# Selective scan on Trainium2: the old y is added by an identity product on TensorE, and ScalarE copies the sum into y

## Chip, cores and metric

One Trainium2 chip, one of its cores. The metric is the device time of one execution in microseconds. Engines are named as in the profile: PE is TensorE (PEld its weight loads), DVE is VectorE, ACT is ScalarE, POOL is GpSimd, SP is SyncE, which issues DMAs.

## What is computed

The program is a vision network of two layers over an image batch (2, 64, 64, 128). Layer 0 holds a convolution and four selective scans over 4096 positions and 256 channels with 16 states; layer 1 holds linear attention and a spectral filter. Only the scans are touched by the change:

```python
def step(h, inp):
    ut, dt, bt, ct = inp
    dA = jnp.exp(dt[..., None] * A4)
    h = dA * h + (dt * ut)[..., None] * bt[:, :, None, :]
    y = jnp.einsum('bkdn,bkn->bkd', h, ct)
    return (h, y)
...
y = out_y[:, 0] + inv_y[:, 0] + wh_y + invwh_y      # four orders summed back in place
```

Of the four scan orders (k = 0 to 3), k = 0 and 2 go over the rows of windows, k = 1 and 3 over the columns; k = 2 and 3 run backward. What each yields is added to one y of 256 channels by 4096 positions (two halves t of 128 channels, on 128 partitions).

## The kernel before

The scans of one image (function `scans`) run over k = 0 to 3 and over 8 chunks of L = 512 positions: 32 chunks an image, 64 in all. `chunk_stream` writes out the first and the last chunk of each k and loops over the others in pairs; every engine runs the same sequence of chunks with a body of its own, and semaphores alone tie them together. In a chunk there are 16 steps n, one for each state, with two halves t:

- ScalarE makes the decay of step n+2 (`decays`, L658) in its iteration n, as soon as VectorE has scanned step n, and every other iteration the scaled x of step n+3 (`times_b`, L649).
- TensorE drives step n+2 into the bank `p_drive` (`drive`: eight turns, L540, where n is even; eight products with a diagonal, L542, where it is odd), then adds what POOL has read out of step n-3 to the bank `p_y` (`sum_y`, L553).
- VectorE scans (`scan`, L762): state = decay * state + drive, 512 positions an instruction.
- POOL multiplies the state by C (`times_c`, L726) and keeps the carry (L730).

The work between chunks is strewn over these iterations. For the next chunk: TensorE projects at n = 0 (`project`, L496), makes the step products at n = 2 (L514), turns B at n = 9 (`turn_b`, L506) and x at n = 10 and 11 (L525); ScalarE takes the projection at n = 1, makes the step's parts at n = 4 (`step_parts`, L631 and L632), exp and ln at n = 6 (L636, L640); VectorE ends the step behind half of scan 8 (`finish_step`, L752); POOL multiplies it by u behind step 8 (L717).

For the chunk before: ScalarE copies its finished `p_y` to `y_tok` at n = 3 (`keep_y`, L672). TensorE turns its two halves into the bank `p_b`, half 0 at n = 6 and half 1 at n = 7 (`turn_y`, L567), each ahead of the drive of that iteration. There is one bank `p_b`: half 1 is turned only when half 0 has been taken out, and `turn_b` of the next chunk uses the same bank after that. VectorE takes the halves out (`add_y`, L777): y = y + bank, for half 0 behind scan (7, 0), for half 1 behind scan (9, 0). In k = 1 and 3 y is reached with a step of 64 positions (256 bytes), since the chunk lies along columns. The last chunk of an image (`c.last`) is ended behind its own steps. `begin_y` (L747) fills y with the skip terms ahead of the first scan and counts `y_begun`.

The semaphores that matter below: `y_kept` (keep_y is done), `y_turned` (a half is in the bank), `y_added` (the bank has been taken out), `scanned`, `driven`, `scaled`, `summed`, `read_out`.

Of the kernel before, what the change touches and what calls it, by code (L numbers as in the profile page):

```python
# [11 lines left out]
ALU = mybir.AluOpType  # L12
ACT = mybir.ActivationFunctionType
ds = bass.ds

P = 128
NB, H, W, C = 2, 64, 64, 128
# [5 lines left out]
L = 512  # L23
# [3 lines left out]
START = 16  # L27
# [372 lines left out]
def scans(nc, m, b):  # L400


    s = m.sem_b
    with ExitStack() as ctx:
# [13 lines left out]
        y_tok = sb("y_tok", [P, NB4, DI])  # L418
        carry = sb("carry", [P, NS, DT2])
        p_prep = ps("p_prep", [P, L])  # L420
        p_b = ps("p_b", [P, L])
# [10 lines left out]
        def flip(ap, c):  # L432
            return ap[:, ::-1] if c.backward else ap

        def following(c, nxt, n):
            return (c, n) if n < NS else (nxt, n - NS)

# [53 lines left out]
        def _(pe):  # L491
# [66 lines left out]
            def turn_y(c, t):  # L558

                if t == 0:  # L560
                    pe.wait_ge(s["y_kept"], START + c.g + 1)
                    pe.wait_ge(s["step_max"], START + c.g * 2 + (2 if c.last else 6 if c.following else 4))
                    pe.wait_ge(s["b_kept"], START + c.g + (1 if c.last else 2))
                else:
                    pe.wait_ge(s["y_added"], START + c.g * 2 + 1)
                for i in range(NB4):
                    last = pe.transpose(p_b[:, i * P:i * P + P], y_tok[:, i, t * P:t * P + P], m.ident[:, :])  # L567
                last.then_inc(s["y_turned"], 1)

            def body(c, nxt):  # L570
# [38 lines left out]
        @block.scalar  # L609
        def _(act):  # L610
            def keep_projection(c):
                act.wait_ge(s["projected"], START + c.g + 1)
                act.wait_ge(s["step_mm"], START + c.g * 2)
                act.wait_ge(s["b_turned"], START + c.g)
                act.wait_ge(s["c_stored"], START + c.g * 32)
                act.copy(xd[:, :], p_prep[:, :]).then_inc(s["xd_kept"], 1)

            def keep_b(c):
                act.wait_ge(s["b_turned"], START + c.g + 1)
                rows = p_b[:, :].rearrange("p (i r) -> p i r", r=P)[:, :, B_ROW:B_ROW + NS]  # L620
                act.copy(b_tok[:, c.parity, :, :], rows).then_inc(s["b_kept"], 1)

            def step_parts(c):
                if not c.first:
                    act.wait_ge(s["decay"], START + c.q * 2 + -2 * NS)
                act.wait_ge(s["x_turned"], START + c.g * 2)
                for t in range(DT2):
                    act.wait_ge(s["step_mm"], START + c.g * 2 + (t + 1))
                    bias = m.dt_b[:, DT2 * c.k + t:DT2 * c.k + t + 1]
                    bank = (p_prep, p_b)[t]  # L630
                    act.activation(softplus[:, t, :], bank[:, :], ACT.Abs, bias=bias).then_inc(s["step_abs"], 1)  # L631
                    act.activation(step[:, c.parity, t, :], bank[:, :], ACT.Relu, bias=bias).then_inc(s["step_max"], 1)  # L632

            def step_exp(c):
                act.wait_ge(s["step_abs"], START + c.g * 2 + 2)
                act.activation(softplus[:, :, :], softplus[:, :, :], ACT.Exp, scale=-1.0).then_inc(s["step_exp"], 1)  # L636

            def step_ln(c):
                act.wait_ge(s["step_exp"], START + c.g + 1)
                act.activation(softplus[:, :, :], softplus[:, :, :], ACT.Ln, bias=1.0).then_inc(s["step_ln"], 1)  # L640

            def times_b(c, n):
                if n == 0:
                    act.wait_ge(s["b_kept"], START + c.g + 1)
                    act.wait_ge(s["x_kept"], START + c.g * 2 + 2)
                if not (c.first and n < 2):
                    act.wait_ge(s["driven"], START + c.q * 2 + (2 * n - 2))
                for i in range(NB4):
                    last = act.activation(scaled[:, i, :], xu_tok[:, c.parity, i, :], ACT.Copy,  # L649
                                          scale=b_tok[:, c.parity, i, n:n + 1])  # L650
                last.then_inc(s["scaled"], 1)

            def decays(c, n, t):
                if n == 0:
                    act.wait_ge(s["step"], START + c.g + 1)
                if not (c.first and n < 2):
                    act.wait_ge(s["scanned"], START + c.q * 2 + (2 * n - 4 + t + 1))
                act.activation(decay[:, n % 2, t, :], step[:, c.parity, t, :], ACT.Exp,  # L658
                               scale=m.a_neg[:, DT2 * c.k + t, n:n + 1]).then_inc(s["decay"], 1)

            def keep_x(c, half):
                act.wait_ge(s["x_turned"], START + c.g * 2 + (half + 1))
                if not c.first:
                    act.wait_ge(s["scaled"], START + c.g * ODD + -ODD)
                    act.wait_ge(s["driven"], START + c.q * 2 + -2 * NS)
                act.copy(xu_tok[:, c.parity, 2 * half:2 * half + 2, :],
                         p_prep[:, :].rearrange("p (i d) -> p i d", d=DI)).then_inc(s["x_kept"], 1)

            def keep_y(c):
                act.wait_ge(s["summed"], START + c.q + NS)  # L670
                act.wait_ge(s["y_turned"], START + c.g * 2)
                act.copy(y_tok[:, :, :], p_y[:, :, :]).then_inc(s["y_kept"], 1)  # L672

            act.preload_act_table_set("natural_log_exp_and_others")
            preparation = {1: keep_projection, 4: step_parts, 11: keep_b}

            def body(c, nxt):
                if c.first:
                    keep_projection(c)
                    step_parts(c)  # L680
                    keep_b(c)
                    step_exp(c)
                    step_ln(c)
                    keep_x(c, 0)
                    keep_x(c, 1)
                    times_b(c, 0)
                    for n in range(2):
                        decays(c, n, 0)
                        decays(c, n, 1)
                    times_b(c, 2)  # L690
                for n in range(NS):
                    of, at = following(c, nxt, n + 2)
                    if of:
                        decays(of, at, 0)
                        decays(of, at, 1)
                    of, at = following(c, nxt, n + 3)
                    if of and at % 2 == 0:
                        times_b(of, at)
                    if n == 3 and not c.first:
                        keep_y(Before(c))  # L700
                    if nxt and n in preparation:
                        preparation[n](nxt)
                    if nxt and n == 6:
                        step_exp(nxt)
                        step_ln(nxt)
                    if nxt and n in (10, 12):
                        keep_x(nxt, n // 2 - 5)
                if c.last:
                    keep_y(c)

            chunk_stream(act, b, body)

        @block.gpsimd
# [29 lines left out]
        def _(dve):  # L743
# [19 lines left out]
                                       flip(p_drive[:, n % 2, t, :], c), 0.0 if c.start else carry[:, n, t:t + 1],  # L763
                                       ALU.mult, ALU.add).then_inc(s["scanned"], 1)

            def add_y(c, t):

                dve.wait_ge(s["y_turned"], START + c.g * 2 + (t + 1))
                dve.wait_ge(s["y_added"], START + c.g * 2 + t)
                dve.wait_ge(s["y_begun"], START + b * 2 + 2)  # L770
                if c.k % 2 == 0:
                    y, p = m.y[:, t, ds(c.at, L)], p_b[:, :]
                else:
                    column = (c.at // W)
                    y = m.y[:, t, :].rearrange("p (h w) -> p w h", w=W)[:, ds(column, L // H), :]
                    p = p_b[:, :].rearrange("p (w h) -> p w h", h=H)
                dve.tensor_tensor(y, y, p, ALU.add).then_inc(s["y_added"], 1)  # L777

            def body(c, nxt):
                if c.first:  # L780
                    begin_y(0)
                    finish_step(c)
                    begin_y(1)
                for n in range(NS):
                    scan(c, n, 0)
                    if n in (7, 9) and not c.first:
                        add_y(Before(c), n // 2 - 3)
                    if nxt and n == 8:
                        finish_step(nxt)
                    scan(c, n, 1)  # L790
                if c.last:
                    add_y(c, 0)
                    add_y(c, 1)

            chunk_stream(dve, b, body)


# [1289 lines left out]
```

## Time and profile before

| | us |
|---|---|
| median of 3 runs (6186.34 to 6195.12) | 6189.54 |
| the profiled execution | 6196.9 |
| span of the profiled execution, first to last instruction | 6195.1 |
| PE busy | 5676.1 (92%) |
| DVE busy | 4384.0 (71%) |
| ACT busy | 3169.3 (51%) |
| POOL busy | 3095.3 (50%) |

The span covers all of the program; the two images' scans lie at about 210 to 1650 us and 1910 to 3340 us, the spectral filter behind them takes most of the rest. Shares over the span are means over these stages, so the scan is read by itself below. In the views, a line of a timeline gives the start, the duration, the engine, the line of the program, the operation, output and inputs, the number of instructions that were merged, and in brackets the idle time ahead of it with what ended it. Durations of merged instructions overlap a little with the next line, so lengths are taken from start to start.

### The profile page before, as it was taken

The page shows a single profiled execution, that of the slowest core. Times are in us where ns is not written, and L with a number is a line of the kernel's source. Part 1 is how long each engine was busy: PE and PEld are TensorE (multiplying, and loading weights), DVE is VectorE, ACT ScalarE, POOL GpSimd, SP SyncE. Part 2 cuts the span into 40 slices and gives each one's busy share as a digit, 9 for nine tenths or more (in the row PEclk, how much of TensorE's full clock was granted, in tenths as well). Part 3 has the DMA queues.
Part 4 walks back from the last instruction along what each step waited for, and adds up shares of the span by engine and source line. Part 5 has one row for each costly group of instructions (what it writes and reads, how often), then busy time and mean ns, then how long its engine had stood idle before and what let it go on. Part 6 is the DMA issues. An engine that isn't in the chain of part 4 may idle for free. (4 is left out here: it accounts for less than half of the span.)

```text
span 6195.1 us, 128742 instructions
## 1 busy us (share of the span) xinstructions
PE 5676.1 (92%) x41691; PEld 5066.6 (82%) x41691; DVE 4384.0 (71%) x5986; ACT 3169.3 (51%) x6029; POOL 3095.3 (50%) x2015
## 2 busy tenths in 40 slices
PE   7899999999888999999998667999999989999998
PEld 5688888888766888888886546999989879999987
DVE  2699999999717999999996664555555555555554
ACT  2699888988737998899886321111111111111110
POOL 1699999999717999999996301111111101111110
PEclk9899999999998999999999888999999999999999
DMA  2455555555414555555554237777766666777765
GB/s 97 109 145 141 141 140 142 140 145 141 128 60 121 143 145 139 139 144 144 142 141 123 56 99 173 156 152 151 152 153 154 167 152 149 154 155 159 153 151 146
DMA packets 1098946, 858.33 MB, mean 139 GB/s; under 512 B 305622, under 2 KB 1021238, under 8 KB 1064374
## 3 DMA queue, kind: packets, MB, share of 16 engines
q1 hardware_dynamic: 1097974, 844.72, 55.1%
q10 hardware_dynamic: 720, 10.49, 0.4%
q8 instruction: 130, 2.13, 0.1%
q14 instruction: 122, 1.00, 0.1%
HBM read 811.50 MB, written 43.55 MB: 138 GB/s over the span
## 5 line engine op out<-in xcount | busy, mean ns | idle before, releaser
L726 POOL TENSOR_TENSOR read<-state,c_wide 128x1024 f32<-128x1024 f32 x1024 | 2419.9, 2380 | 216.7 <-DVE state L762 129.0
L762 DVE TENSOR_TENSOR_SCAN state<-decay,carry,p_drive 128x512 f32<-128x512 f32 x1792 | 2140.9, 1259 | 103.9 <-PE p_drive L540 57.1
L658 ACT ACTIVATE decay<-step,a_neg 128x512 f32<-128x512 f32 x2048 | 1398.2, 717 | 225.1 <-DVE state L762 215.9
L1747 PE MATMUL p_y<-window,x_high 128*128 128x256 f32 x7936 | 1490.8, 286 | 0.0
L1811 ACT COPY term_blocks<-p_s 128x256 f32<-128x256 f32 x832 | 310.5, 373 | 2096.2 <-PE p_s L1747 2096.2
L1747 PEld LDWEIGHTS p_y<-window,x_high 128*128 128x128 f32 x7936 | 1239.1, 191 | 0.0
L1747 PE MATMUL p_y<-window,x_low 128*128 128x256 f32 x3968 | 1130.5, 285 | 0.0
L553 PE MATMUL p_y<-ident,read 128*128 128x128 f32 x8192 | 1064.1, 273 | 13.0 <-ACT y_tok L672 3.7
L542 PE MATMUL p_drive<-diag_b,xu_tok 128*128 128x128 f32 x8192 | 1004.0, 276 | 1.3 <-DVE state L762 1.3
L542 PEld LDWEIGHTS p_drive<-diag_b,xu_tok 128*128 128x128 f32 x8192 | 960.5, 193 | 1.6 <-DVE state L762 1.6
L553 PEld LDWEIGHTS p_y<-ident,read 128*128 128x128 f32 x8192 | 925.2, 141 | 25.4 <-issue 21.7
L649 ACT ACTIVATE scaled_x<-xu_tok,b_tok 128x256 f32<-128x256 f32 x2048 | 868.1, 496 | 74.9 <-PE p_drive L540 74.7
L1747 PEld LDWEIGHTS p_y<-window,x_low 128*128 128x128 f32 x3968 | 755.8, 190 | 0.0
L1842 POOL TENSOR_TENSOR mix_weights<-mix_weights,frac_filter 128x512 f32<-128x512 f32 x64 | 73.2, 1144 | 1318.3 <-PE p_mix L1785 1311.0
L540 PE MATMUL p_drive<-ident,scaled_x 128*128 128x128 f32 x4096 | 562.2, 278 | 114.6 <-ACT scaled_x L649 97.2
L540 PEld LDWEIGHTS p_drive<-ident,scaled_x 128*128 128x128 f32 x4096 | 452.8, 142 | 254.4 <-issue 144.6
L1747 PE MATMUL p_s<-window,x_high 128*128 128x256 f32 x2432 | 531.6, 306 | 80.6 <-DMA window<-taps_scratch 45.4
L1880 DVE TENSOR_TENSOR term_blocks<-p_y,term_blocks 128x512 f32<-128x512 f32 x384 | 265.6, 692 | 391.0 <-PE p_y L1747 383.4
L1834 POOL TENSOR_TENSOR mix_weights<-mix_weights 128x512 f32<-128x512 f32 x64 | 82.5, 1290 | 893.0 <-DMA mix_weights<-in_M_minus 890.5
L1747 PEld LDWEIGHTS p_s<-window,x_high 128*128 128x128 f32 x2432 | 390.3, 191 | 136.0 <-issue 97.1
L1785 PE MATMUL p_mix<-term_blocks,mix_weights 128*128 128x512 f32 (+1 forms) x1280 | 461.2, 507 | 1.9 <-DVE term_blocks L1863 1.9
L1862 DVE TENSOR_TENSOR term_blocks<-p_y,term_blocks 128x256 f32<-128x256 f32 x448 | 186.3, 416 | 356.5 <-PE p_y L1747 355.4
(257 smaller groups left out, 6023.7 us busy)
## 6 DMA issues: line engine op xcount, KB each, us to landing
c_wide<-c_scratch SPq DMA_DIRECT2D x256, 1024.0 KB, 4.7
window<-taps_scratch SPq DMA_DIRECT2D x576, 257.0 KB, 6.5
diag_b<-diag_scratch SPq DMA_DIRECT2D x256, 512.0 KB, 4.1
window<-taps_scratch SPq DMA_DIRECT2D x768, 129.0 KB, 5.3
window<-taps_scratch SPq DMA_DIRECT2D x128, 513.0 KB, 7.1
window<-taps_scratch SPq DMA_DIRECT2D x64, 385.0 KB, 6.1
gate_scratch<-gate_out SPq DMA_DIRECT2D x16, 512.0 KB, 3.1
gate_in<-gate_scratch SPq DMA_DIRECT2D x8, 1024.0 KB, 6.0
```

The lines of the kernel that those rows point to most:

```text
L540: last = pe.transpose(o, scaled[:, i, t * P:t * P + P], m.ident[:, :])
L542: last = pe.matmul(o, xu_tok[:, c.parity, i, t * P:t * P + P], diag[:, n // 4 % 2, n // 2 % 2, i, :], start=True, stop=True)
L553: last = pe.matmul(p_y[:, i, t * P:t * P + P], read[:, n % 4, t, i * P:i * P + P], m.ident[:, :], start=n == 0 and i % 2 == 0 and t == 0, ...
L649: last = act.activation(scaled[:, i, :], xu_tok[:, c.parity, i, :], ACT.Copy, scale=b_tok[:, c.parity, i, n:n + 1])
L658: act.activation(decay[:, n % 2, t, :], step[:, c.parity, t, :], ACT.Exp, scale=m.a_neg[:, DT2 * c.k + t, n:n + 1]).then_inc(s["decay"], 1)
L726: pool.tensor_tensor(read[:, n % 4, :, :], state[:, n % 4, :, :], wide, ALU.mult).then_inc(s["read_out"], 1)
L762: dve.tensor_tensor_scan(flip(state[:, n % 4, t, :], c), flip(decay[:, n % 2, t, :], c), flip(p_drive[:, n % 2, t, :], c), 0.0 if c.start ...
L1747: last = pe.matmul(out, x[:, source, blk, :], view[:, :, at:at + P][:, :, ::-1], start=first and x is m.x_high and z == 0, stop=True, skip ...
L1785: last = pe.matmul(p_mix[par][:, at:at + size], mix_now[:, kind, reach, :], filtered[:, j % 2, par ^ kind, kind, at:at + size], start=kind ...
L1811: act.copy(shared[:, i % 4, :, :], shared_bank(i)).then_inc(s["kept"], 1)
L1862: dve.tensor_tensor(to[:, :, 0:P], half_of(p_y[i % 4], 0), shared[:, i % 4, :, :], ALU.add)
L1880: dve.tensor_tensor(to.rearrange("p k (h t) -> p k h t", h=2), p_y[i % 4][:, :].rearrange("p (h k t) -> p k h t", h=2, k=2), out.rearrange ...
```

## The change

On TensorE `turn_y` puts the old y into the bank first, as a product with the identity (one 128x128 by 128x512 product, start of the accumulation), and the four turns then accumulate onto it. ScalarE gets a new function `end_y`, which copies the bank into y, in its iterations n = 7 and n = 8 behind decays and `times_b`. VectorE's `add_y` is gone with its two calls. The meaning of `y_added` stays (the bank has been taken out), but ScalarE counts it now. `y_of` is the address of a chunk's half in y.

```diff
+        def y_of(c, t):
+
+            if c.k % 2 == 0:
+                return m.y[:, t, ds(c.at, L)]
+            column = (c.at // W)
+            return m.y[:, t, :].rearrange("p (h w) -> p w h", w=W)[:, ds(column, L // H), :]
...
             def turn_y(c, t):
...
                 else:
                     pe.wait_ge(s["y_added"], START + c.g * 2 + 1)
+                pe.wait_ge(s["y_begun"], START + b * 2 + 2)
+                old = y_of(c, t)
+                bank = p_b[:, :] if c.k % 2 == 0 else p_b[:, :].rearrange("p (w h) -> p w h", h=H)
+                pe.matmul(bank, m.ident[:, :], old, start=True, stop=False, skip_group_check=True)
                 for i in range(NB4):
-                    last = pe.transpose(p_b[:, i * P:i * P + P], y_tok[:, i, t * P:t * P + P], m.ident[:, :])
+                    last = pe.matmul(p_b[:, i * P:i * P + P], y_tok[:, i, t * P:t * P + P], m.ident[:, :], start=False,
+                                     stop=True, is_transpose=True, skip_group_check=True)
                 last.then_inc(s["y_turned"], 1)
...
+            def end_y(c, t):
+
+                act.wait_ge(s["y_turned"], START + c.g * 2 + (t + 1))
+                src = p_b[:, :] if c.k % 2 == 0 else p_b[:, :].rearrange("p (w h) -> p w h", h=H)
+                act.copy(y_of(c, t), src).then_inc(s["y_added"], 1)
...
                     if n == 3 and not c.first:
                         keep_y(Before(c))
+                    if n in (7, 8) and not c.first:
+                        end_y(Before(c), n - 7)
...
                 if c.last:
                     keep_y(c)
+                    end_y(c, 0)
+                    end_y(c, 1)
...
-            def add_y(c, t):
-
-                dve.wait_ge(s["y_turned"], START + c.g * 2 + (t + 1))
-                dve.wait_ge(s["y_added"], START + c.g * 2 + t)
-                dve.wait_ge(s["y_begun"], START + b * 2 + 2)
...
-                dve.tensor_tensor(y, y, p, ALU.add).then_inc(s["y_added"], 1)
...
                 for n in range(NS):
                     scan(c, n, 0)
-                    if n in (7, 9) and not c.first:
-                        add_y(Before(c), n // 2 - 3)
                     if nxt and n == 8:
                         finish_step(nxt)
                     scan(c, n, 1)
-                if c.last:
-                    add_y(c, 0)
-                    add_y(c, 1)
```

## Rows read from the trace of the kernel before

**Rows 1.** Busy us and count of PE, PEld, DVE, ACT, POOL; clock; DMA: scan stretch

```profile
215.00:580.00 365.00, 349.21 (x2820) 316.33 (x2820) 338.14 (x285) 329.03 (x613) 340.19 (x204) 0.99 0.52 141
```

**Rows 2.** Timeline of VectorE: its first sums of chunks 1 and 31

```profile
278.04 0.69 DVE L777 TENSOR_TENSOR y<-y,p_b 128x512 f32 x1 [0.72 <-PE p_b L567]
...
1623.33 1.33 DVE L777 TENSOR_TENSOR y<-y,p_b 128x512 f32<-128x512 f32 x1 [0.77 <-PE p_b L567]
```

**Rows 3.** Timeline of ScalarE in one chunk of k=0

```profile
402.31 1.70 ACT L649 ACTIVATE scaled_x<-xu_tok,b_tok 128x256 f32<-128x256 f32 x4 [1.18 <-PE p_drive L540]
...
415.67 1.69 ACT L649 ACTIVATE scaled_x<-xu_tok,b_tok 128x256 f32<-128x256 f32 x4
417.26 1.58 ACT L658 ACTIVATE decay<-step,a_neg 128x512 f32<-128x512 f32 x2
...
446.67 1.71 ACT L649 ACTIVATE scaled_x<-xu_tok,b_tok 128x256 f32<-128x256 f32 x4 [1.18 <-PE p_drive L540]
```

**Rows 4.** Timeline of TensorE in the same chunk

```profile
411.40 1.09 PE L540 MATMUL p_drive<-ident,scaled_x 128*128 128x128 f32 x8 [0.43 <-ACT scaled_x L649]
412.32 1.04 PE L553 MATMUL p_y<-ident,read 128*128 128x128 f32 x8
413.19 0.60 PE L567 MATMUL p_b<-ident,y_tok 128*128 128x128 f32 x4
413.63 1.95 PE L542 MATMUL p_drive<-diag_b,xu_tok 128*128 128x128 f32 x16
415.42 1.04 PE L553 MATMUL p_y<-ident,read 128*128 128x128 f32 x8
417.49 1.31 PE L540 MATMUL p_drive<-ident,scaled_x 128*128 128x128 f32 x8 [1.03 <-ACT scaled_x L649]
...
419.89 0.66 PE L506 MATMUL p_b<-ident,xd 128*128 128x128 f32 x4 [0.22 <-DVE y L777]
420.38 1.95 PE L542 MATMUL p_drive<-diag_b,xu_tok 128*128 128x128 f32 x16
...
437.42 1.88 PE L496 MATMUL p_prep<-s,xproj 128*128 x4
439.13 1.04 PE L540 MATMUL p_drive<-ident,scaled_x 128*128 128x128 f32 x8
```

**Rows 5.** Groups by shape, whole span: VectorE's sums; busy us, mean ns, idle before

```profile
L777 DVE TENSOR_TENSOR y<-y,p_b 128x512 f32 x96 | 94.7, 986 | 33.7 <-PE p_b L567 33.7
...
L777 DVE TENSOR_TENSOR y<-y,p_b 128x512 f32<-128x512 f32 x32 | 31.3, 979 | 22.9 <-PE p_b L567 22.9
```

**Rows 6.** Timeline of VectorE in the chunk of rows 3, end of the step

```profile
414.57 2.33 DVE L752 TENSOR_TENSOR step<-step,shared 128x1024 f32<-128x1024 f32 x1 [0.23 <-ACT shared L640]
```

**Rows 7.** Groups, whole span: ScalarE's copies out of a bank; busy us, mean ns

```profile
L666 ACT COPY xu_tok<-p_prep 128x512 f32<-128x512 f32 x128 | 72.4, 566 | 29.4 <-PE p_prep L525 29.4
...
L314 ACT ACTIVATE s<-pc,conv_b 128x512 f32 x32 | 36.1, 1129 | 0.0
...
L312 ACT ACTIVATE s<-pc,conv_b 128x512 f32 x32 | 22.0, 688 | 110.3 <-PE pc L285 110.2
```

**Rows 8.** One line, 580 to 940 us (k=1): duration ns min/median/max, starts

```profile
L777 DVE TENSOR_TENSOR y<-y,p_b x16: 656/1262/1360, 588.5 to 914.5; 128x512 f32 x12, 128x512 f32<-128x512 f32 x4
```

**Rows 9.** Columns of rows 1: pauses of TensorE and the 5 us after

```profile
3389.36:3392.65 3.29, 0.00 (x1) 0.00 (x1) 1.63 (x2) 1.52 (x2) 2.73 (x2) 1.00 0.20 59
3392.65:3397.65 5.00, 4.10 (x32) 3.72 (x32) 1.29 (x2) 0.00 (x0) 2.25 (x1) 1.00 0.23 66
...
3502.72:3506.47 3.75, 0.00 (x0) 0.00 (x1) 3.75 (x21) 2.50 (x5) 1.54 (x2) 1.00 0.00 0
3506.47:3511.47 5.00, 5.00 (x27) 4.53 (x28) 2.35 (x12) 0.32 (x2) 0.96 (x1) 0.66 0.00 0
...
3764.22:3769.17 4.95, 0.00 (x0) 0.03 (x1) 3.97 (x5) 0.00 (x0) 4.46 (x6) 0.73 0.86 147
3769.17:3774.17 5.00, 5.00 (x26) 5.00 (x27) 0.71 (x3) 0.40 (x2) 0.40 (x1) 0.59 0.99 271
```

More of the change, by code:

```diff
@@ L764, in scan @@
                                        ALU.mult, ALU.add).then_inc(s["scanned"], 1)
-            def add_y(c, t):
-                dve.wait_ge(s["y_turned"], START + c.g * 2 + (t + 1))
-                dve.wait_ge(s["y_added"], START + c.g * 2 + t)
-                dve.wait_ge(s["y_begun"], START + b * 2 + 2)
[L771 to L776, printed above, removed]
-                dve.tensor_tensor(y, y, p, ALU.add).then_inc(s["y_added"], 1)
             def body(c, nxt):
```

## The prediction

> **What bounds the kernel now.** I read first the busy time by engine inside the scan, then the length of one chunk, then one chunk in order of time on each engine. The busy times name no single bound: in a 365 us stretch of the scan TensorE is busy 349 us, POOL 340, VectorE 338 and ScalarE 329 [rows 1]. So a gain on VectorE isn't a gain by itself. VectorE's first sum of the first chunk starts at 278.04 and that of the thirty-first at 1623.33, which makes 44.84 us for a chunk [rows 2].
>
> The order of time shows a ring. In a chunk of stage k=0, ScalarE can start `times_b` of step 6 at 402.31, when TensorE has driven step 4; from there it runs without a pause (times_b, keep_y, decays, step_parts, decays, times_b, decays, exp, ln, decays, times_b) until 417.26, 14.95 us [rows 3]. TensorE waits for the end of that: its drive of step 10 starts at 417.49 with a wait of 1.03 us on ScalarE. Then come sum_y, turn_b and, from 420.38, the drive of step 11 and all that follows without any pause worth naming [rows 4], until the next chunk's drive of step 4 lets ScalarE start `times_b` of step 6 again, at 446.67 [rows 3]. So a round is 14.95 us of ScalarE, 3.12 us in between (417.26 to 420.38) and 26.29 us of TensorE (420.38 to 446.67): 44.36 us. Every link is a semaphore or the order on one engine. VectorE is in the ring only for a moment: `turn_b` waits for its second sum, 0.22 us [rows 4].
>
> **What leaves VectorE.** 128 sums, 94.7 + 31.3 = 126.0 us, and the waits ahead of them, 33.7 + 22.9 = 56.6 us [rows 5]. At most 183 us would come back if VectorE were the ring. It isn't: after the first sum VectorE runs two scans and then waits for ScalarE's ln, 0.23 us [rows 6]; without the sum it arrives earlier and waits longer. I count the removal at 0 and what hides it is ScalarE's 14.95 us.
>
> **What the identity products cost.** Nothing in the trace multiplies the identity by 512 columns, but `project` does two full 128x128 by 128x512 products between 437.42 and 439.13, 0.86 us each [rows 4]. Two a chunk. The first, in `turn_y(0)`, falls ahead of drive 8, for which TensorE waits 0.43 us for ScalarE now [rows 4]: 0.86 - 0.43 = 0.43 us of delay, and that is absorbed, because TensorE waits for ScalarE a little later in any case. Without that cover it would be 0.86 x 60 = 52 us. The second is in the ring (below).
>
> **What the copies cost on ScalarE.** The copy of 128x512 out of a bank is 0.57 us [rows 7]. In the stages k=1 and 3 it writes y with a step of 256 bytes. The nearest row for a stepped write is the second Silu, which writes the column order and takes 1.129 us where the first, from the same bank, takes 0.688 [rows 7]: +0.44 us. VectorE's sum read and wrote with that step and cost no more at its quickest, 0.656 us in k=1 against 0.69 in k=0 [rows 2, 8]. I take +0.44 for ScalarE (between 0 and 0.88) and 0 for the product's reading of the old y (between 0 and +0.86, a doubling). The Trainium skill's page "SBUF — State Buffer" (section "Door 1: The DMA port swizzle") says that a step beyond 16 bytes loses bandwidth on each access. ScalarE's rows agree with that, VectorE's do not; by the rule the product pays too, which is the upper end just named.
>
> **The wait that the change puts in.** This is the term that decides. `turn_y(1)` has to wait until the bank is free. Before, VectorE freed it right after scan 7: at 413.19 TensorE starts the second turn without a wait and does drive 9 (413.63 to 415.42) and sum_y 4 while ScalarE is still busy [rows 4]. After, the bank is freed by `end_y(0)`, which stands in ScalarE's program behind decays and `times_b` of step n=7, so at 417.26, the end of the 14.95 us. TensorE is in order: behind its wait stand drive 9, sum_y 4, drive 10, sum_y 5, turn_b, drive 11. Worked out on the same chunk, from 417.26:
> copy 0.57 [rows 7], semaphore 0.13 (as from the end of `times_b`, 415.67 + 1.69, to drive 10 at 417.49) [rows 3, 4], product 0.86, four turns 0.44 (413.19 to 413.63), drive 9 1.79, sum_y 4 0.87 (412.32 to 413.19), drive 10 0.87 (eight transposes as well), sum_y 5 0.87, turn_b 0.49 (419.89 to 420.38) [rows 4]. Sum 6.89 us in place of 3.12. The round becomes 14.95 + 6.89 + 26.29 = 48.13 us. Who waits behind it: VectorE's scan 9 (needs drive 9), POOL's step 8 (needs sum_y 4, some 3.6 us later than now), then everybody.
>
> Against the mean of 44.84 that is +3.29 us a chunk. Thirty chunks of each of the two images have the full round: +197 us. Of these 60, 28 belong to k=1 or 3: 28 x 0.44 = +12. The last chunk and the two closing turns of each image have the products without the ring; I put +5 for all of that.
>
> **TensorE's clock.** The new wait makes TensorE idle from the end of sum_y 3 (413.19 now, about 413.6 with the first product ahead of it) to 417.96: 4.4 us a chunk, more where the copy is stepped. In the scan the granted clock is 0.99 of full [rows 1]. Elsewhere in this trace TensorE had such pauses: after 3.75 us without a product the clock of the next 5 us was 0.66, after 4.95 us it was 0.59, while after 3.29 us it stayed 1.00 [rows 9]. The 0.66 is a stretch at 1.2 GHz among 2.4 GHz. A clock of 0.66 over 5 us of dense work loses 5 x 0.34 = 1.7 us, 0.59 loses 2.05. Whatever is lost there lies in the ring, right behind the wait. I take 1.7 us: 60 x 1.7 = +102 us, with bounds 0 and 60 x 2.05 = 123. The Trainium skill's page "TensorE: Matmul & The Clock Gate" (section "HAM oscillation — how this bites in real kernels") tells of a kernel that waits between bursts and is throttled anew in every round, which speaks against this change. The rows named agree with it, except that no scan chunk here has had such a pause yet.
>
> **The sum.** 197 + 12 + 5 + 102 = +316 us. The profiled execution took 6196.9 us, so 6513; it lies 7.4 us above the median of the runs, so 6189.5 + 316 = 6505 us.
>
> **Rivals.**
> Clock stays up: the pause is there but the clock holds, as after 3.29 us [rows 9]. Then 197 + 12 + 5 = 214, 6404 us; without the stepped write 6392. For it: the pause of 3.29 us kept the clock. Against it: ours lies between the two that lost it. Chance 0.19.
> The wait is hidden (the other side): if ScalarE reached `end_y(0)` before TensorE has finished sum_y 3, that is 4 us earlier than its rows say, the ring would be as now and TensorE's own work would decide: 349.2/365 x 44.84 = 42.9 us [rows 1] and two products of 0.86, 44.6 us a chunk, -0.2 x 60 = -14 us, 6175 us. It decides from the point where the 14.95 us shrink below 11. Nothing on ScalarE is removed, so I see no way: 0.03 for it and 0.02 for a mixture that ends within 0.2%.
> Stepped accesses are dear: product at four times 0.86 in the second turn, 2.6 x 28 = +72, and the copy at +0.88, another +12: 6589 us. Chance 0.06. For it: ScalarE's stepped write; against it: VectorE's sums.
> Smaller slowdown, under 6385: ScalarE's stretch or TensorE's 26.29 us has slack which the rows don't show. Chance 0.03.
> The forecast itself: 0.67.
>
> **How the numbers follow.** The range goes from 6385 (clock holds, no stepped write, 6392, less the spread of the runs) to 6590 (clock 123, the product doubled in the stepped chunks +24, the copy +25, semaphores of 0.3 us more a round +18, from 6189.5 + 202: 6582). Outside remain the two cases of hidden waits, the smaller slowdown and a part of the dear accesses. About 0.2% can be told from no change here: faster by over that 0.03, within it 0.02, slower 0.95.
>
> **What would show it.** In the profile after: TensorE's second turn (the product on the identity ahead of the turns) waits some 4 us for ScalarE's copy into y in nearly every chunk; that copy starts without a pause behind `times_b`; a chunk lasts 49 to 51 us by its copies; granted clock in the scan 0.95 to 0.97 instead of 0.99, low right behind the wait; VectorE idle 8 us or more a chunk, with drive 9 as the releaser. A chunk of 48.1 us at full clock would be the first rival. The forecast is wrong if TensorE's wait ahead of the second turn is under 2 us, or if the chunks stay near 44.8 us: then ScalarE doesn't run without pause up to `end_y(0)`, and the ring isn't what I read.

## The result and the profile after

The change makes the kernel slower: 6565.3 us (median of four runs, 6564.6 to 6572.2) against 6189.8 (four runs, 6186.3 to 6195.1). The ratio is 1.061, 95% interval 1.059 to 1.062. The profiled execution took 6572.2 us where the one of before took 6196.9: +375.3 us. The forecast was +316 us, 6505 us in a range of 6385 to 6590.

The busy time of the engines over the whole span, in the profile after (us, share of the span, count):

```profile
PE 5925.9 (90%) x41947; PEld 5228.4 (80%) x41947; DVE 4331.5 (66%) x5858; ACT 3272.6 (50%) x6157; POOL 3094.2 (47%) x2015
```

TensorE has 128 products (256 records) more and is busy 250 us longer, far more than 128 products of 0.86 us = 110 us. The stretches of time, in the columns of [rows 1], first the stretch of the scan, then five pieces of one chunk of k=0:

```profile
215.00:580.00 365.00, 335.00 (x2554) 299.93 (x2553) 300.23 (x243) 302.01 (x562) 304.21 (x183) 0.94 0.48 125
...
418.85:430.21 11.36, 11.25 (x97) 10.47 (x94) 10.56 (x9) 11.10 (x20) 10.31 (x7) 1.00 0.88 140
430.21:434.76 4.55, 0.17 (x2) 0.01 (x1) 3.74 (x3) 4.52 (x10) 3.48 (x2) 0.90 0.21 58
434.76:437.48 2.72, 2.72 (x7) 1.58 (x7) 0.33 (x1) 1.10 (x2) 0.00 (x0) 0.50 0.69 289
437.48:440.77 3.29, 3.29 (x17) 3.29 (x17) 1.18 (x1) 0.59 (x1) 0.00 (x0) 0.52 0.00 0
440.77:443.83 3.06, 3.06 (x31) 3.06 (x29) 2.75 (x4) 2.26 (x5) 1.94 (x1) 1.00 0.00 0
```

Every engine does less in 365 us than in [rows 1], since fewer chunks fit into the stretch. In the chunk, TensorE has almost nothing to do for 4.55 us, and then works without a gap for 6.01 us (434.76 to 440.77) at a granted clock of 0.50 to 0.52, that is 1.2 GHz in place of 2.4.

What TensorE waits for there stands in its timeline of the same chunk (start, duration, line, operation, count, and in brackets the idle time ahead and what ended it):

```profile
427.17 1.02 PE L576 MATMUL p_b<-y,ident 128*128 x2
428.03 0.60 PE L578 MATMUL p_b<-ident,y_tok 128*128 128x128 f32 x4
428.46 1.04 PE L547 MATMUL p_drive<-ident,scaled_x 128*128 128x128 f32 x8
429.34 1.04 PE L560 MATMUL p_y<-ident,read 128*128 128x128 f32 x8
434.76 2.07 PE L576 MATMUL p_b<-y,ident 128*128 x2 [4.38 <-ACT y L685]
436.62 1.06 PE L578 MATMUL p_b<-ident,y_tok 128*128 128x128 f32 x4
437.48 3.46 PE L549 MATMUL p_drive<-diag_b,xu_tok 128*128 128x128 f32 x16
...
443.83 1.95 PE L549 MATMUL p_drive<-diag_b,xu_tok 128*128 128x128 f32 x16
```

and ScalarE's, from `times_b` of step 6 in this chunk to the same instruction in the next:

```profile
419.11 1.71 ACT L661 ACTIVATE scaled_x<-xu_tok,b_tok 128x256 f32<-128x256 f32 x4 [1.13 <-PE p_drive L547]
...
432.46 1.69 ACT L661 ACTIVATE scaled_x<-xu_tok,b_tok 128x256 f32<-128x256 f32 x4
434.06 0.56 ACT L685 COPY y<-p_b 128x512 f32 x1
...
437.81 0.59 ACT L685 COPY y<-p_b 128x512 f32 x1 [1.95 <-PE p_b L578]
...
470.15 1.70 ACT L661 ACTIVATE scaled_x<-xu_tok,b_tok 128x256 f32<-128x256 f32 x4 [1.15 <-PE p_drive L547]
```

In [rows 4] the second turn at 413.19 started without a wait. Now the product ahead of it stands 4.38 us for ScalarE's copy, and the copy starts at 434.06 without a pause behind `times_b`, 14.95 us after 419.11. From the copy to drive 11 it is 9.77 us (434.06 to 443.83), where before it was 3.12 from the end of `times_b`. From there to the next `times_b` of step 6 it is 26.32 us; before it was 26.29.

The table of waits of the whole program, three of its lines (who waits at which line, for what; us in total, count, longest):

```profile
POOL read L748 <- PE p_y L560: 566.0, 246, 8.1
DVE state L784 <- PE p_drive L549: 278.5, 138, 5.2
...
PE p_b L576 <- ACT y L685: 256.4, 64, 4.4
```

TensorE's wait occurs ahead of the second half of all 64 chunks, 4.0 us in the mean. The waits of VectorE for the drives and of POOL for `p_y` are for the most part the same delay, seen by those who stand behind TensorE.

### The profile page after: what moved, and what is told of

Read it like the earlier page. It is cut to its first block and busy times, and to the rows that moved or that the text cites. A ratio compares the mean times of both kernels' runs of the same rounds, so it can differ in the third digit from the quotient of the medians.

```text
span 6570.4 us, 129250 instructions
## 1 busy us (share of the span) xinstructions
PE 5925.9 (90%) x41947; PEld 5228.4 (80%) x41947; DVE 4331.5 (66%) x5858; ACT 3272.6 (50%) x6157; POOL 3094.2 (47%) x2015
## 5 line engine op out<-in xcount | busy, mean ns | idle before, releaser
L784 DVE TENSOR_TENSOR_SCAN state<-decay,carry,p_drive 128x512 f32<-128x512 f32 x1792 | 2167.3, 1264 | 503.3 <-PE p_drive L549 251.4
L549 PE MATMUL p_drive<-diag_b,xu_tok 128*128 128x128 f32 x8192 | 1077.1, 288 | 0.0
L549 PEld LDWEIGHTS p_drive<-diag_b,xu_tok 128*128 128x128 f32 x8192 | 1039.5, 206 | 0.0
L1751 PE MATMUL p_s<-window,x_high 128*128 128x256 f32 x2432 | 530.7, 306 | 81.6 <-DMA window<-taps_scratch 46.4
L547 PE MATMUL p_drive<-ident,scaled_x 128*128 128x128 f32 x4096 | 541.4, 275 | 9.8 <-ACT scaled_x L661 8.7
L576 PE MATMUL p_b<-y,ident 128*128 (+1 forms) x256 | 224.3, 968 | 259.1 <-ACT y L685 256.4
```

Of the source, the lines that this page charges most:

```text
L547: last = pe.transpose(o, scaled[:, i, t * P:t * P + P], m.ident[:, :])
L549: last = pe.matmul(o, xu_tok[:, c.parity, i, t * P:t * P + P], diag[:, n // 4 % 2, n // 2 % 2, i, :], start=True, stop=True)
L576: pe.matmul(bank, m.ident[:, :], old, start=True, stop=False, skip_group_check=True)
L784: dve.tensor_tensor_scan(flip(state[:, n % 4, t, :], c), flip(decay[:, n % 2, t, :], c), flip(p_drive[:, n % 2, t, :], c), 0.0 if c.start ...
L1751: last = pe.matmul(out, x[:, source, blk, :], view[:, :, at:at + P][:, :, ::-1], start=first and x is m.x_high and z == 0, stop=True, skip ...
```

## Experiments

Two theories to begin with. **The place of the copy**: the one bank `p_b` couples TensorE's second product to `end_y(0)`, which ScalarE reaches only at the end of its 14.95 us; the low clock follows from that wait. **The work**: 128 products and 128 copies were put on engines that had none to spare, and would cost the same wherever they stood. The chunks below are measured from one copy of `p_y` into `y_tok` to the next. The columns by k give the commonest length, the means are over 30 chunks of the first image, and the last column is the interval ahead of its closing copy. The ratios are to runs of the kernel before taken beside each run (medians of 6188.3 to 6192.9 us). In the kernel after, the first, the thirty-first and the closing one of these copies in ScalarE's timeline:

```profile
269.32 0.99 ACT L690 COPY y_tok<-p_y 128x1024 f32<-128x1024 f32 x1
...
1795.29 0.99 ACT L690 COPY y_tok<-p_y 128x1024 f32<-128x1024 f32 x1
1835.55 1.01 ACT L690 COPY y_tok<-p_y 128x1024 f32<-128x1024 f32 x1 [10.37 <-PE p_y L560]
```

(1795.29 - 269.32) / 30 = 50.87 us, and 1835.55 - 1795.29 = 40.3. Not all chunks of the kernel after have the commonest length: some are 49.4 to 50.9 us.

| kernel | us | ratio to before (95%) | chunk, k=0, 2 | chunk, k=1, 3 | mean | last |
|---|---|---|---|---|---|---|
| before | 6189.8 | | 44.4 | 45.6 | 44.85 | 33.8 |
| after | 6565.3 | 1.061 (1.059 to 1.062) | 51.1 | 51.15 | 50.87 | 40.3 |
| fill_pause | 6446.8 | 1.041 (1.040 to 1.043) | 48.2 | 49.5 | 48.76 | 39.2 |
| no_product | 6474.2 | 1.045 (1.044 to 1.047) | 48.9 and 50.1 | 49.0 and 50.1 | 49.56 | 36.2 |
| vector_copies | 6256.2 | 1.011 (1.009 to 1.013) | 45.0 | 46.4 | 45.76 | 35.8 |
| early_copy | 6203.7 | 1.002 (1.001 to 1.003) | 44.5 | 45.4 | 44.88 | 37.9 |
| two_banks | 6204.4 | 1.002 (1.001 to 1.003) | 44.5 | 45.4 | 44.89 | 38.1 |
| before_two_banks | 6190.9 | 1.000 (0.999 to 1.001) | 44.4 | 45.6 | 44.87 | 33.8 |
| late_second_sum | 6190.4 | 1.000 (0.999 to 1.001) | 44.4 | 45.6 | 44.87 | 33.7 |
| pool_step_first | 6189.2 | 1.000 (0.999 to 1.001) | 44.4 | 45.6 | 44.84 | 33.7 |
| two_banks_pool_first | 6166.3 | 0.996 (0.994 to 0.997) | 44.0 | 45.0 | 44.38 | 36.2 |

In no_product a shorter and a longer chunk mostly follow each other by turns, whatever the k; why was not traced.

**fill_pause: keep TensorE at work in the pause.** Behind sum_y 3 TensorE does four products into `p_prep`, which is free there; nothing reads them.

```diff
+ if n == 6 and not c.first:
+     for i in range(4):
+         pe.matmul(p_prep[:, :], m.ident[:, :], y_tok[:, 0:2, :], start=True, stop=True)
```

> The changed kernel, with four more products of 128x512 on TensorE (identity times y_tok, 0.86 us each, into the bank p_prep that is free then) behind sum_y 3 of n=6, in the pause ahead of the second turn; nothing reads what they write. Theory (the pause lets the clock fall, and that costs 2.9 us a chunk behind the pause): the clock in the scan goes back to 0.98 or more, the stretch from the copy to drive 11 shrinks from 9.8 us to about 6.9 in k=0; chunks of 48.1 us in k=0 and 2, 49.4 in k=1 and 3; 6189 + 197 + 12 + 24 + 5 = 6430 us, 6400 to 6460. Rival (TensorE has too much work, the clock is only a sign of it): more work makes it slower still, 6565 us or above.

Measured: 6446.8 us, 118 us less than after, with more work. Stretch of the scan and timeline of TensorE, with the added products first:

```profile
215.00:580.00 365.00, 355.07 (x2685) 308.31 (x2685) 309.89 (x250) 313.57 (x582) 313.33 (x188) 0.99 0.50 131
```

```profile
424.82 3.60 PE L614 MATMUL p_prep<-y_tok,ident 128*128 128x512 f32 x8
...
429.36 1.12 PE L576 MATMUL p_b<-y,ident 128*128 x2 [0.94 <-ACT y L688]
430.32 0.60 PE L578 MATMUL p_b<-ident,y_tok 128*128 128x128 f32 x4
430.76 1.95 PE L549 MATMUL p_drive<-diag_b,xu_tok 128*128 128x128 f32 x16
...
435.60 1.95 PE L549 MATMUL p_drive<-diag_b,xu_tok 128*128 128x128 f32 x16
```

The clock is back at 0.99 and the product takes 0.96 us to the turns in place of 1.86. So the low clock costs 118 us, and the rest of the slowdown, 257 us, is there at full clock. The wait for the copy is still what holds TensorE. The copy starts at 428.66 here and drive 11 at 435.60, 6.94 us later, where the forecast had 6.89; the chunk is 48.2 us, where it had 48.13.

**no_product: the wait without the product.** The turns start the bank, and the old y isn't added; ScalarE copies as in the kernel after.

```diff
- pe.matmul(bank, m.ident[:, :], old, start=True, stop=False, skip_group_check=True)
- last = pe.matmul(p_b[...], y_tok[...], m.ident[:, :], start=False, stop=True, is_transpose=True, ...)
+ last = pe.transpose(p_b[...], y_tok[...], m.ident[:, :])
```

> The changed kernel without the identity products: the four turns start the bank themselves, ScalarE copies the bank into y as before, so y holds only the last order's part at each place (the old y isn't added). Theory (the wait for ScalarE's copy, and the clock behind it, are the cost): the pause stays, some 5.2 us now, and the clock falls all the same; of the 6.1 us a chunk about 1.9 go, the product at half clock: 6440 to 6490 us. Rival (the products themselves are the cost): 6190 to 6250 us.

Measured: 6474.2 us. The second half's turns in the timeline:

```profile
433.60 1.12 PE L575 MATMUL p_b<-ident,y_tok 128*128 128x128 f32 x4 [4.51 <-ACT y L681]
```

The pause is as long without the product (4.51 us; some 5.2 were expected), and three quarters of the slowdown stay (284 of 376 us). Taking the products away gives back 91 us; that they cost this only where they stand behind the wait is seen from the experiments that follow.

**vector_copies: the product without ScalarE's copies.** VectorE copies the bank into y at the two places where it added before.

```diff
- if n in (7, 8) and not c.first: end_y(Before(c), n - 7)          # ScalarE
+ if n in (7, 9) and not c.first: take_y(Before(c), n // 2 - 3)    # VectorE, dve.tensor_copy
```

> The changed kernel with its products, but VectorE copies the bank into y, at the places where its sums stood (behind scan 7 and scan 9 of half 0). Theory: no pause of TensorE above 2 us, the clock stays at 0.99, the ring is that of the kernel before; the two products fill TensorE's 1.5 us of slack a chunk and go a little over it, by 0.3 us in k=0 and 2 and by 1.9 in k=1 and 3, where the stepped product takes 1.70: 6250 us, 6220 to 6290. Rival (products are the cost): 6400 or more. Rival (VectorE's time is what counts): like before, 6190.

Measured: 6256.2 us, 309 us less than after, with all 128 products in it. TensorE's two products of a chunk of k=1 have no wait:

```profile
640.02 1.88 PE L576 MATMUL p_b<-y,ident 128*128 x2
...
643.91 1.88 PE L576 MATMUL p_b<-y,ident 128*128 x2
```

Here it is VectorE's second copy that holds TensorE up, ahead of `turn_b`:

```profile
651.69 0.66 PE L513 MATMUL p_b<-ident,xd 128*128 128x128 f32 x4 [0.58 <-DVE y L787]
```

So the slowdown hangs on who empties the bank, and when. The two experiments that follow leave the work where the change has put it, and take away only the place or only the shared bank.

**early_copy: the first copy one iteration sooner.** `end_y(0)` goes from behind `times_b` at n=7 to n=6, between decays and exp; nothing else changes.

```diff
- if n in (7, 8) and not c.first:
-     end_y(Before(c), n - 7)
+ if n in (6, 8) and not c.first:
+     end_y(Before(c), n // 2 - 3)
```

> The changed kernel with the first copy moved in ScalarE's program from behind times_b of n=7 to n=6, behind its decays and ahead of exp; same work on every engine. Theory: the bank is free when TensorE reaches the second turn, no pause, clock 0.99, and the ring is 44.1 us in k=0 and 2, with TensorE's work (44.6 and, with the stepped product, 46.3) as the bound: 6200 to 6260 us. Rival (ScalarE's added work, or TensorE's, is the cost): stays within 50 us of 6565.

**two_banks: the second half into another bank.** Half 1 goes to `p_prep`, so it needn't wait for the copy of half 0; `turn_b` then waits for the first copy alone and the turn of x for both.

```diff
- pe.wait_ge(s["y_added"], START + c.g * 2 + 1)       # turn_y, t = 1
+ pe.wait_ge(s["y_added"], START + c.g * 2)
...
+ p_half = (p_b, p_prep)[t]
```

> The changed kernel with the second half turned into the bank p_prep, which is free from step_parts to turn_x: the second turn then waits for no copy. turn_b waits for the first copy, turn_x for the second. Theory: the wait itself is gone and with it the pause and the fall of the clock; TensorE's work is the bound, 44.6 us a chunk in k=0 and 2 and 46.3 in k=1 and 3 (stepped product 1.70): 6230 us, 6190 to 6260. Rival (ScalarE's added copies lengthen its stretch): 6300 or more.

Measured: 6203.7 and 6204.4 us, the same within their intervals. TensorE's second product of a chunk of k=0 has no wait, in early_copy and in two_banks:

```profile
413.75 1.02 PE L576 MATMUL p_b<-y,ident 128*128 x2
```

```profile
412.93 1.02 PE L577 MATMUL p_prep<-y,ident 128*128 x2
```

Moving one copy of 0.56 us gives back 362 of the 376 us. The work theory has fallen: products and copies are all still there, and the chunk is 44.9 us as before. In k=1 and 3 it is 45.4 us, where both expectations had put TensorE's work at 46.3. Of what stays, some 14 us, the last chunks of the images make up 6: they are 4.1 to 4.3 us longer in the first image and 1.9 in the second. The rest was not traced.

But why is neither faster than before, with 126 us of sums [rows 5] gone from VectorE? In two_banks TensorE is busy 357 of 365 us in k=0 and 298 of 300 in k=1 (stretches of time):

```profile
215.00:580.00 365.00, 356.99 (x2844) 320.67 (x2844) 331.50 (x271) 334.88 (x626) 340.31 (x204) 0.99 0.54 141
600.00:900.00 300.00, 297.99 (x2331) 261.51 (x2330) 274.64 (x221) 276.89 (x510) 277.91 (x168) 1.00 0.54 140
```

That looks like TensorE at its end. The same question was put to the kernel before, by taking away in turn what TensorE waits for there.

**before_two_banks: the same two banks in the kernel before.** VectorE's sums stay; `turn_b` no longer waits for the second one.

```diff
- pe.wait_ge(s["y_added"], START + (c.g * 2 + -2))    # turn_b
+ pe.wait_ge(s["y_added"], START + (c.g * 2 + -3))
...
+ p_half = (p_b, p_prep)[t]                            # turn_y; add_y reads the same
```

> The kernel before, unchanged but for the banks: the second half is turned into p_prep, turn_b waits for the first sum alone, turn_x for both. Theory (in the kernel before VectorE's second sum is in the ring, by turn_b's wait of 0.2 us in k=0 and 2 and 0.8 in k=1 and 3): 32 x 0.2 + 28 x 0.8 = 29 us less, 6160, 6150 to 6185. Rival (other waits take its place): 6185 to 6195.

**late_second_sum: besides, VectorE's second sum one scan later.**

```diff
- if n in (7, 9) and not c.first: add_y(Before(c), n // 2 - 3)
+ if n in (7, 10) and not c.first: add_y(Before(c), n // 10)
```

> The kernel before with the second half in p_prep, as in before_two_banks, and VectorE's second sum moved from behind scan (9, 0) to behind scan (10, 0), since in before_two_banks TensorE's drive 11 waits 0.70 us for scan 9, which stands behind that sum. Theory (the second sum is in the ring through scan 9): drive 11 starts 0.4 us earlier in k=0 and 2 and up to 1.0 us earlier in k=1 and 3: 32 x 0.4 + 28 x 1.0 = 41 us less, 6150, 6140 to 6175. Rival (POOL's read-out or the next wait takes it): 6180 to 6195, and then VectorE's sums cost nothing where they stand.

**pool_step_first: besides, POOL multiplies the step by u ahead of its eighth read** in place of behind it.

```diff
+ if nxt and n == 8: step_times_u(nxt)
  times_c(c, n)
- if nxt and n == 8: step_times_u(nxt)
```

> late_second_sum with POOL's product of the next step and u taken ahead of its read-out of step 8 instead of behind it. Theory (in late_second_sum TensorE waits 0.4 us for that product ahead of turn_x: a second path, ln, end of the step, scan 8, read-out 8, that product, turn_x, is as long as the one through turn_b; POOL stands idle 1.38 us ahead of read-out 8, so the product fits in there): now both paths are shorter and the 0.4 to 1.0 us a chunk that late_second_sum was to gain appear: 6150 us, 6135 to 6175. Rival (a third path, POOL's own 41 us a chunk or VectorE's scans, takes over at once): 6180 to 6195.

Measured: 6190.9, 6190.4 and 6189.2 us: all three as before. My expectation of a gain missed three times. Each time the wait taken away is gone, and another stands close by. In before_two_banks drive 11 waits for VectorE:

```profile
873.43 1.16 PE L543 MATMUL p_drive<-diag_b,xu_tok 128*128 128x128 f32 x8 [0.70 <-DVE state L763]
```

In late_second_sum that is gone too, and the turn of x waits for POOL's product, which stands behind its read:

```profile
873.10 0.65 PE L526 MATMUL p_prep<-ident,shared 128*128 128x128 f32 x4 [0.40 <-POOL shared L718]
```

In pool_step_first POOL's product comes early. VectorE's second sum stands in the same chunk's timeline without a wait, and VectorE scans on from there for 17.67 us without a pause:

```profile
418.89 2.37 POOL L718 TENSOR_TENSOR shared<-step,s 128x1024 f32<-128x1024 f32 x1
```

```profile
423.33 0.66 DVE L779 TENSOR_TENSOR y<-y,p_prep 128x512 f32 x1
423.91 17.67 DVE L763 TENSOR_TENSOR_SCAN state<-decay,carry,p_drive 128x512 f32<-128x512 f32 x15
```

By these waits, three paths through a chunk are equally long to within a microsecond: ScalarE's stretch and the turns on TensorE; ln, the end of the step, scan 8 and POOL's read and product; and VectorE's own scans and sums. This is read from the waits; no run takes away the third path alone.

**two_banks_pool_first: the same move of POOL in two_banks**, where VectorE's sums are gone as well.

```diff
+ if nxt and n == 8: step_times_u(nxt)                 # POOL, two_banks otherwise
  times_c(c, n)
- if nxt and n == 8: step_times_u(nxt)
```

> two_banks (the changed kernel without the wait) with the same move on POOL. Theory (there TensorE's own work is the bound, 44.5 us a chunk at 98% busy in k=0 and 2 and 45.4 at 99% in k=1 and 3): nothing to gain, 6195 to 6210 us. Rival (POOL's path bounds it too): 6160 to 6185, and then the change can pay.

Measured: 6166.3 us, 38 us less than two_banks and faster than both kernels (0.996, 0.994 to 0.997). The rival won, by which TensorE with 98% of busy time was not yet the bound. TensorE's turn of x, two_banks first:

```profile
422.88 0.65 PE L533 MATMUL p_prep<-ident,shared 128*128 128x128 f32 x4 [0.39 <-POOL shared L741]
```

and two_banks_pool_first:

```profile
419.91 0.60 PE L533 MATMUL p_prep<-ident,shared 128*128 128x128 f32 x4
```

The wait is gone, and in its k=1 TensorE is now busy for all but 0.8 of 300 us. With the wait for the copy and POOL's path out of the way, the change as a whole (VectorE's sums gone, products and copies added) is worth 23 us against pool_step_first (6189.2 to 6166.3). How much VectorE's part alone is worth hangs on what else there is: with the products in place, taking the copies from VectorE to ScalarE's early place gave 52 us (vector_copies to early_copy).

## Why the prediction came out as it did

**The ring: right, to the hundredth in its untouched parts.** ScalarE's 14.95 us, now 419.11 to 434.06, and TensorE's stretch, 26.32 for 26.29, are as read. The step that decides, `end_y(0)` at the end of ScalarE's stretch and TensorE in order behind it, is shown by early_copy: one copy moved, 362 us back.

**The wait, +197 us: right in size.** At full clock the part in between is 6.94 us for 6.89, and the chunk of k=0 is 48.2 for 48.13 (fill_pause). Against the mean of before, (48.2 - 44.85) x 60 = 201. The forecast, too, compared the ring of k=0 with the mean over all k, and so its +197 holds two things that it does not name. Stage by stage the chunk grows by 3.8 us in k=0 (44.4 to 48.2) and 3.9 in k=1 (45.6 to 49.5); 3.8 x 60 = 228. Against that stands the longer ring that k=1 and 3 had before, where VectorE's sums have the step: TensorE waits there for a scan that stands behind the first sum, and longer than in k=0 for the second sum. In a chunk of k=1 of the kernel before:

```profile
868.06 0.66 PE L540 MATMUL p_drive<-ident,scaled_x 128*128 128x128 f32 x4 [0.60 <-DVE state L762]
...
870.40 0.66 PE L506 MATMUL p_b<-ident,xd 128*128 128x128 f32 x4 [0.81 <-DVE y L777]
```

By these waits it is 0.60 + 0.81 - 0.22 = 1.2 us, the 45.6 against 44.4 of the table; with the sums these 28 x 1.2 = 34 us leave the ring, and 228 - 34 = 194.

**The stepped accesses, +12: too small, and one row was misread.** The chunk of k=1 in fill_pause is 1.3 us longer than that of k=0; over 28 chunks that is 36 us. The copy was sized well. The step that failed is the product's reading of the old y with a step, taken as 0 from VectorE's rows with an upper end of a doubling. VectorE's rows do not say 0. The quickest sum of [rows 8], 0.656 us, stands at the head of that window: it is a sum of the last chunk of k=0, which has no step. VectorE's timeline before, with it and the first sum of k=1:

```profile
596.44 0.66 DVE L777 TENSOR_TENSOR y<-y,p_b 128x512 f32<-128x512 f32 x1
632.85 1.35 DVE L777 TENSOR_TENSOR y<-y,p_b 128x512 f32 x1 [0.77 <-PE p_b L567]
```

In the first image VectorE's sums take 0.65 to 0.69 us without the step and 1.24 to 1.36 with it; [rows 2] has one of each. Read so, the row would have given the product about its upper end, 28 x 0.86 = 24 us more. It is a doubling for TensorE as well. Timeline of TensorE in a chunk of k=1 of the kernel after, first product and second:

```profile
731.28 1.88 PE L576 MATMUL p_b<-y,ident 128*128 x2
732.98 0.62 PE L578 MATMUL p_b<-ident,y_tok 128*128 128x128 f32 x4
...
739.32 2.07 PE L576 MATMUL p_b<-y,ident 128*128 x2 [3.98 <-ACT y L685]
741.21 1.04 PE L578 MATMUL p_b<-ident,y_tok 128*128 128x128 f32 x4
```

From start to start the first takes 1.70 us; in k=0 it took 0.86 (427.17 to 428.03). The Trainium skill's page "SBUF — State Buffer", section "Door 1: The DMA port swizzle", has every access that goes on to a new line of 16 bytes pay a penalty. TensorE's 1.70 us at full clock, ScalarE's copies and VectorE's sums agree with it, against what the forecast says of VectorE.

**The clock, +102: the mechanism right, the term too small and its shape wrong.** fill_pause shows 118 us between the two kernels, and by the chunks (50.87 - 48.76) x 60 = 127. The forecast put 1.7 us into every chunk. In chunks of the commonest length it is 2.9 in k=0 (51.1 - 48.2) and 1.65 in k=1 (51.15 - 49.5), and over all chunks 2.1 in the mean. The granted clock of the scan is 0.94, where the forecast had 0.95 to 0.97. For k=0 the failing step was to take the deficit from stretches of 5 us [rows 9]. The low clock lies on TensorE's work from 434.76 to 440.77, and that work takes 6.01 us where the same instructions take 0.86 + 0.44 + 1.79 = 3.09 at full clock. In other chunks the clock comes back sooner. One of the soonest behind an unstepped product, kernel after, columns as in [rows 1], the product with its turns and then drive 9:

```profile
587.99:590.71 2.72, 2.72 (x6) 1.58 (x7) 0.41 (x1) 1.18 (x2) 0.00 (x0) 0.50 0.73 304
590.71:592.55 1.84, 1.84 (x17) 1.84 (x17) 0.53 (x1) 0.59 (x1) 0.00 (x0) 0.97 0.00 0
```

For k=1 the stepped product hides part of the loss: at 1.2 GHz it takes 1.89 us (739.32 to 741.21), and that is hardly more than the 1.86 of the unstepped one (434.76 to 436.62). So the step and the low clock do not add up there: in the kernel after itself the product's step costs the ring next to nothing, as forecast, but by luck, since it is the low clock that hides it.

**The ends, +5: too small.** The last interval of an image is 40.3 us for 33.8, twice 6.5 = 13. There the copies and turns stand one behind the other; early_copy still has 4.1 of the 6.5 in the first image and 1.9 in the second.

Together by the chunks: 201 + 36 + 127 + 13 = 377, measured 376. By the runs themselves fill_pause splits it as 257 + 118; the chunks would have 250 + 127. Of the difference of some 8 us, 1.4 lie in the last interval of fill_pause's second image (41.7 us, where after has 40.3); the rest I didn't trace.

**VectorE's sums, counted at 0: right in k=0, for a wider reason.** I gave ScalarE's 14.95 us as what hides them; in k=1 and 3 the sums put the 1.2 us named above into the ring of before, which the mean as base took in unnamed. The experiments on the kernel before show that POOL's path and VectorE's own hide as well, within a microsecond. That `turn_b` waits 0.22 us for the second sum had no price either: with that wait gone (before_two_banks) nothing changed.

**The rivals.** "Clock stays up" is fill_pause, where it was forced: 6447, not 6404. The stepped product (28 x 0.84 = 24) and the ends (5.3 and 7.9, forecast 5) account for 32 of the 43 us; the rest I didn't trace. "The wait is hidden" is early_copy and two_banks: 6204, not 6175, as TensorE's busy time does not decide while POOL's product still holds up the turn of x. With that out of the way it is 6166, under the 6175 that TensorE's busy time was taken to allow.

## What to carry to other kernels

When a step goes to another in-order engine, look first at which instruction frees the buffer that it shares, and at the place of that instruction in its engine's order: one copy of 0.56 us, one iteration too late, cost 362 us, and a free bank or an earlier place gave them back. Here TensorE's waits of 3.9 to 4.4 us cost more than their length, since the work behind them was done at the lower clock; price that by the work that lies in the low stretch. Before a minimum or a median of a window is used as a price, look at which instruction it belongs to: a window that began one chunk too early made a doubled access look free. Where removing a wait brings nothing, the next path is as long: remove waits together, and don't take 98% of busy time for the bound before the last wait is gone.

## What the runs showed of the hardware

- TensorE's clock was 0.50 behind pauses of 3.9 to 4.4 us in the scan and full again some 3 to 6 us after the work had started anew, so it was lost in every chunk. The Trainium skill's page "TensorE: Matmul & The Clock Gate", section "HAM oscillation — how this bites in real kernels", tells of a kernel that waits between bursts and is throttled each round; the trace agrees. Four products that nobody reads, in the pause, were worth 118 us.
- An fp32 identity product of 512 columns that reads its moving data with a step of 256 bytes took 1.70 us against 0.86 at 2.4 GHz, but 1.89 against 1.86 at 1.2 GHz (kernel after, 739.32 to 741.21 and 434.76 to 436.62).
- VectorE's sum of a bank and y took 1.24 to 1.36 us where it reads and writes y with that step and 0.65 to 0.69 where it doesn't (kernel before); its copy, which only writes with the step, 1.01 to 1.08 against 0.66 to 0.69 (vector_copies).
- ScalarE's copy out of a bank took 1.01 us where it writes with that step and 0.59 where it doesn't (kernel after):

```profile
738.17 1.01 ACT L685 COPY y<-p_b 128x512 f32 x1
```
